# Two edits to a graph-plus-LSTM kernel: the short item chunk as one stacked pass, and a fourth input pass between the two groups' state matmuls

## The reference

```
x = x + relu(adj @ (item_feat @ W_item.T + b_item) + layernorm(x) @ W_user.T + b_user)
h = lstm(layernorm(x))                      # 10000 steps in the reference, 128 wide, 4 gates
g = argmax(h @ W_lin.T + b_lin)             # 0 or 1 for each row
w = g * h;  inc = cumsum(w)
x = x + 2*h + (inc - w) * fw_att + (inc[-1] - inc) * bw_att
```

## Time and profile before

| | |
|---|---|
| median of 3 runs | 1486.9 us (1485.9 to 1490.18) |
| the profiled execution, its own time | 1486.99 us |
| its span, first to last instruction | 1485.2 us |
| granted TensorE clock over the span | 0.990 |
| PE busy | 1449.2 us (98%) |
| DVE busy | 1218.3 us (82%) |
| ACT busy | 1088.3 us (73%) |
| DMA moved | 426.67 MB, mean 287 GB/s |
| stage 1 (PE's last `psG` pass starts) | to 1169.8 us |
| stage 2 and the closing sums | the rest |

### The profile page before, as it was taken

One profiled execution on the slowest core, in us unless ns is written; L12 is line 12 of the kernel. 1 busy time (PEld: TensorE's weight loads), 2 busy tenths in 40 slices (PEclk: granted clock), 3 DMA queues, 4 the chain that ended last, 5 costly groups with the idle time before them and its releaser, 6 DMA issues.

```text
span 1485.2 us, 25012 instructions
## 1 busy us (share of the span) xinstructions
PE 1449.2 (98%) x7584; PEld 1227.4 (83%) x7584; DVE 1218.3 (82%) x2027; ACT 1088.3 (73%) x1601; POOL 212.8 (14%) x189
## 2 busy tenths in 40 slices
PE   8999999999999999999999999999999799999994
PEld 7878888788778888888888888877888699999994
DVE  7998888888888888888888888888888566677677
ACT  5778777778777778777777787777778476556662
POOL 0000010000001001001001000000100032017775
PEclk9999999999999999999999999999999899999997
DMA  9889999999999999999999999999999203000003
GB/s 382 309 325 359 376 345 360 367 350 365 358 352 361 370 351 363 371 356 358 367 352 371 352 359 376 340 369 355 350 363 380 97 1 123 15 2 0 0 0 139
DMA packets 70515, 426.67 MB, mean 287 GB/s; under 512 B 8723, under 2 KB 17620, under 8 KB 70358
## 3 DMA queue, kind: packets, MB, share of 16 engines
q1 hardware_dynamic: 68896, 425.12, 76.6%
q10 hardware_dynamic: 1590, 1.18, 0.2%
HBM read 416.02 MB, written 10.24 MB: 287 GB/s over the span
## 4 chain that ended last, share of the span: by engine, by line
issue 79%; PE 19%; DVE 1%; POOL 0%; ACT 0%; POOLq 0%; DVEq 0%
PE psZ L848 10%; PE psZ L836 3%; PE psZ L837 2%; PE psZ L838 2%; PE psZ L854 1%; DVE u L1241 1%; PE psZ L824 0%; PE psZ L914 0%; POOL rstd L419 0%; POOLq L422 0%; ACT normed L557 0%; PE psZ L918 0%; DVE dif L1256 0%; PE psV L734 0%; DVE dif L1254 0%
## 5 line engine op out<-in xcount | busy, mean ns | idle before, releaser
L998 DVE TENSOR_TENSOR a_lo<-raw,a_hi 128x1000 fp32r<-128x1000 f32 (+1 forms) x800 | 917.3, 1182 | 108.4 <-ACT a_hi L586 101.9
L586 ACT ACTIVATE a_hi<-raw 128x1000 fp32r<-128x1000 f32 (+1 forms) x800 | 806.2, 1030 | 253.7 <-PE psG L759 170.6
L757 PE MATMUL psG<-a_hi,item_hi 128*128 128x500 f32 (+1 forms) x1580 | 635.5, 402 | 2.5 <-DVE a_lo L998 1.6
L759 PE MATMUL psG<-a_hi,item_lo 128*128 128x500 f32 (+1 forms) x1580 | 615.6, 390 | 0.0
L758 PE MATMUL psG<-a_lo,item_hi 128*128 128x500 f32 (+1 forms) x1580 | 612.2, 387 | 0.0
L757 PEld LDWEIGHTS psG<-a_hi,item_hi 128*128 128x128 f32 (+1 forms) x1580 | 296.4, 188 | 81.1 <-DVE a_lo L998 16.7
L759 PEld LDWEIGHTS psG<-a_hi,item_lo 128*128 128x128 f32 (+1 forms) x1580 | 297.7, 188 | 61.1
L758 PEld LDWEIGHTS psG<-a_lo,item_hi 128*128 128x128 f32 (+1 forms) x1580 | 297.3, 188 | 60.7 <-issue 4.4
L419 POOL TENSOR_TENSOR rstd<-var,minus_half 125x4 f32<-125x4 f32 x40 | 76.2, 1905 | 1096.8 <-DVE var L982 1096.8
L848 PE MATMUL psZ<-hist,wh 128*128 (+1 forms) x1264 | 169.8, 277 | 0.1
L848 PEld LDWEIGHTS psZ<-hist,wh 128*128 128x128 f32 x1264 | 154.0, 191 | 2.1 <-issue 0.6
(11 more groups left out here) (143 smaller groups left out, 809.4 us busy)
## 6 DMA issues: line engine op xcount, KB each, us to landing
raw<-in_adj_main SPq DMA_DIRECT2D x360, 1000.0 KB, 6.9
raw<-in_adj_main SPq DMA_DIRECT2D x40, 750.0 KB, 4.2
x_copy<-xb SPq DMA_DIRECT2D x20, 250.0 KB, 5.5
u<-x_copy SPq DMA_DIRECT2D x1, 5000.0 KB, 14.8
out<-u SPq DMA_DIRECT2D x25, 200.0 KB, 2.4
xb<-in_xT SPq DMA_DIRECT2D x18, 250.0 KB, 5.3
u<-in_itemT SPq DMA_DIRECT2D x8, 512.0 KB, 11.7
u<-in_itemT SPq DMA_DIRECT2D x1, 648.0 KB, 12.5
```

What stands on the lines that cost most here:

```text
L586: nc.scalar.activation(a_hi[:, s % CUT, 0:n], raw[:, r % RAW, at:at + n], ACT.Copy)\
L757: pe.matmul(bank, w_hi, hi, start=(c == 0), stop=False)
L759: last = pe.matmul(bank, w_lo, hi, start=False, stop=(c == CH))
L998: dve.tensor_tensor(a_lo[:, s % CUT, 0:n], raw[:, r % RAW, at:at + n], a_hi[:, s % CUT, 0:n].bitcast(f32), ALU.subtract).then_inc(lo_ready, 1)
```

## The change

Part one, the short chunk. The DMA of its 16 rows is issued three times, to partitions 0, 32 and 64 (`STACK`). ACT rounds all of them as before. DVE splits only the full chunk into `a_lo`, and then, on partitions 32 to 47, overwrites the rounded values by the rests. The item weights of the chunk are laid out the same way once, in block 0: high part on partitions 0 and 32, low part on 64, zeros between. PE then does one pass over 80 partitions, in which the three products add up by themselves, in place of three passes over 16.

Part two, the LSTM. The twelve input passes become a list; four of them, instead of three, stand between the state matmuls of group 0 and group 1, and eight instead of nine after those of group 1.

More of the change, by code:

```diff
@@ L134, in program @@
         bi_row = sb("bi_row", [1, HID], f32, first)
+        item_tail = sb("item_tail", [P, STACKED], f32, first)
         item_lo = sb("item_lo", [P, (CH + 1) * HID], f32r, first)
@@ L200, in program @@
         wi_in = sem("wi_in")
+        item_tail_ready = sem("item_tail_ready")
         bi_in = sem("bi_in")
@@ L420, in inv_std @@
                                    ALU.pow).then_inc(ln_rstd, 1)
-            with nc.gpsimd.Fori(0, 2 * NB) as m:
+            inv_std(0)
[5 more added lines that the diff above has]
+            with nc.gpsimd.Fori(1, 2 * NB) as m:
                 inv_std(m)
@@ L797, in item_quad @@
                     pe.wait_ge(item_sum, q - 1)
+                if q == QUADS - 1:
+                    pe.wait_ge(item_tail_ready, 1 + len(STACK))
                 for c in range(4 * q, min(4 * q + 4, CH + 1)):
-                    rows = P if c < CH else TAIL
-                    last = pe.matmul(psI[0:rows, q % 2, (c % 4) * HID:(c % 4 + 1) * HID],
-                                     u[:, L + c * P:L + c * P + rows], wi[:, :], start=True, stop=True)
+                    rows = P if c < CH else STACKED
+                    columns = u[:, L + c * P:L + (c + 1) * P] if c < CH else item_tail[:, :]
+                    last = pe.matmul(psI[0:rows, q % 2, (c % 4) * HID:(c % 4 + 1) * HID], columns, wi[:, :],
+                                     start=True, stop=True)
                 last.then_inc(item_psum, 1)
@@ L835, in from_input @@
                     z = psZ[:, 2 * par + q // 2, (q % 2) * XC:(q % 2 + 1) * XC]
-                    pe.matmul(z, w_hi, hi, start=(q % 2 == 0), stop=False, skip_group_check=True)
-                    pe.matmul(z, w_hi, lo, start=False, stop=False, skip_group_check=True)
-                    pe.matmul(z, w_lo, hi, start=False, stop=False, skip_group_check=True)
+                    if part == 0:
+                        pe.matmul(z, w_hi, hi, start=(q % 2 == 0), stop=False, skip_group_check=True)
+                    if part == 1:
+                        pe.matmul(z, w_hi, lo, start=False, stop=False, skip_group_check=True)
+                    if part == 2:
+                        pe.matmul(z, w_lo, hi, start=False, stop=False, skip_group_check=True)
             def from_state(n, g, row, par):
@@ L878, in lstm_pair @@
                          logit=lambda: logits(2 * i + half, par, half))
-            pe.wait_ge(prep, 14)
+            pe.wait_ge(prep, 17)
             pe.wait_ge(u_ready, NB)
@@ L1014, in item_sum_part @@
                 dve.wait_ge(prep, 1)
-                for c0, c1, rows in ((0, n - 1, P), (n - 1, n, TAIL)):
-                    dve.tensor_tensor(sq[0:rows, c0 * HID:c1 * HID].rearrange("p (c h) -> p c h", h=HID),
-                                      psI[0:rows, q % 2, c0 * HID:c1 * HID].rearrange("p (c h) -> p c h", h=HID),
-                                      bi[0:rows, :].unsqueeze(1).to_broadcast([rows, c1 - c0, HID]), ALU.add)\
-                        .then_inc(item_sum if rows == TAIL else prep, 1)
-                dve.wait_ge(prep, 2)
+                for c0, c1, a, b in ((0, n - 1, 0, P), *((n - 1, n, a, a + TAIL) for a in STACK)):
+                    dve.tensor_tensor(sq[a:b, c0 * HID:c1 * HID].rearrange("p (c h) -> p c h", h=HID),
+                                      psI[a:b, q % 2, c0 * HID:c1 * HID].rearrange("p (c h) -> p c h", h=HID),
+                                      bi[a:b, :].unsqueeze(1).to_broadcast([b - a, c1 - c0, HID]), ALU.add)\
+                        .then_inc(item_sum if a == STACK[-1] else prep, 1)
+                dve.wait_ge(prep, 4)
             def item_lo_part(q):
```

27 lines of the change are left out of this document (14 added, 13 removed).

## The result

The changed kernel takes 1474.64 us in the median of four runs (1470.58 to 1476.14), the kernel before 1488.02 (1485.9 to 1490.18): ratio 0.9906, 95% interval 0.988 to 0.9931. Forecast were 1470.6, range 1464 to 1480. The profiled execution took 1475.1 us with a span of 1473.2, against 1486.99 and 1485.2 before: 11.9 us less, 16.4 were forecast. The main mechanism came as forecast, but the sum holds one gain that wasn't foreseen and four losses that were missed or put too small.

What follows compares the result with a forecast made beforehand. PE's own passes were taken to set the pace. Stage 1 (16.0 saved, 0.8 and 1.0 lost: -14.2) and the LSTM (-2.2) took 1486.99 us to 1470.6, range 1464 to 1480.

Steps and rivals of the forecast that it cites:

- The block end, 0.84 us: End of each block: one 80-row pass replaces three 16-row ones, saving PE 0.84 us a block, 16.0 over 19.
- rival (a): Block end: 80 rows still cost the change of rows, 8.6 us saved instead of 16.0, total 1478.0; chance 0.15.
- I price it at nothing: Two added short-chunk DMAs a block: landing at most 0.55 us later, covered by a 0.83 us margin, no cost.
- rival (d): Block end: the two added small DMAs lag 1.05 us each, 0.43 lost a block, total 1493.8; chance 0.05.
- I take 1.0 us over all blocks as loss (bounds 0 and 5): Stage 1, nearly full DMA engines: PE's waits for DVE splits grow, costing 1.0 us over all blocks.
- 0.5 later. Enough.: Next block's first DVE split ends at 714.10, PE would arrive at 714.62, 0.5 us later; no new wait.
- Rival (c): Stage 1: the DMA queue is the real bound, blocks keep 56.70 us plus 0.18, total 1489.0; chance 0.07, part included.
- 0.8 us, bounds 0.4 and 1.2: Block 0: added DVE work (two adds, the operation on own_hi, the split in two) costs 0.8 us.
- block 0's 0.84 is lost: Join to block 1: PE already waits 1.42 us for DVE's first split, so block 0's 0.84 us saves nothing.
- The fourth input pass: LSTM loop: fills a 0.10 us stall in group 1's state matmuls (S1); step 3.33 to 3.23, 2.2 us gained.
- From the first logits on nothing moves: LSTM second half: state is ready over 0.7 us before group 0's state matmuls (S0), so steps gain nothing.
- Rival (b): LSTM loop: no slack behind group 0's state matmuls (S0); 1.6 us slower instead of 2.2 faster, total 1474.4; chance 0.09.

Runs made afterwards that it cites:

- The run with the weight operations moved: Changed kernel with VectorE's twelve operations on the weights moved from block 0's end to pieces 12 to 17 of the last block: 1470.8 us, ratio 0.9886.

## Why the prediction was right, and which terms were off

**The block end, 0.84 us: right.** 80 rows run like 128, and rival (a) falls. The 0.84 is 2 x 0.225 for two passes and 0.39 for the change of rows; taken apart, two passes are 0.48 a block (56.07 with three stacked passes, 55.59 with one) and the change of rows 0.33 to 0.39 (the old passes over 80 rows, the stacked one over 48 and 64).

**Not foreseen: 0.27 us a block inside the blocks,** 19 x 0.27 = 5.1 us. All four kernels with PE's old passes at the block end (before, the loads alone, the four passes alone, the old passes over 80 rows) have 0.2267 to 0.2269 between passes; all nine with the stacked pass have 0.2256 or 0.2257, with one pass or three, 48 rows or 80. Not the number of passes, not the rows, not the added loads. What is left is all that the nine share: where instructions stand in a program, VectorE's last split, which is cut in two, GpSimd's added work, and the place of the tiles in SBUF, for the change allocates a new tile `item_tail`, 320 bytes a partition, ahead of `item_lo`, `raw`, `a_hi` and `a_lo`. That the pattern of distances comes back with each turn of the rings `a_hi` and `a_lo` would fit the last; no run tests it. The cause stays open.

**"I price it at nothing" (the two added DMAs): right.** Alone they change nothing measurable, and rival (d) falls. ACT's wait for the short chunk grew by 0.6 us, a little over the 0.55 allowed. The trace counts 64 more packets a block, not 32, half of them under 512 bytes. The 2.0 us that the prediction takes from the Trainium skill, "DMA: Bandwidth & Descriptors", Anatomy of one DMA, stand there for DMAs that GpSimd issues. These are SyncE's, and whatever fixed time they have, two more of them a block cost the run nothing: it isn't serial in the queue.

**"I take 1.0 us over all blocks as loss (bounds 0 and 5)": this is the step that failed most.** It measured 7.5 us (4 to 11 by the other profiles of this stage). The prediction worked out that 1.7 us of each block were free in the queue and that 0.84 + 0.18 would fit. It was 1.11 + 0.18, and above all a free mean is not a free queue: with less time per block, the loads are late more often, mostly at the same places of the block. ACT's waits for loads went from 67 to 123 us while its waits for PE fell from 158 to 97; with 5% fewer bytes the two turned back. "0.5 later. Enough." for the first split of the next block left 0.17 us over the 0.35 that was known to be enough, and in 5 of 18 block ends that split came late, by 0.1 to 0.2 us. Rival (c), that the queue keeps blocks at 56.70, is wrong as it stood, for many blocks take 55.59; but its mechanism holds for part of the gain.

**"0.8 us, bounds 0.4 and 1.2" (block 0): mis-sized.** It measured 1.5. Of this 1.3 us are shown in the rows: the two added sums cost 0.6 and not 0.4, the operation on `own_hi` 0.4 and not 0.3, the split in two 0.2 and not 0.1. And "block 0's 0.84 is lost" left out what a longer wait does to PE: the clock fell, 1.5 us more in block 1. The run with the weight operations moved takes away both the wait and the fall.

**The fourth input pass: right.** Forecast were S1 with 1.05, S0 to S1 1.37, S1 to S0 1.86, the step 3.23 and 2.2 us in all; measured were 1.05, 1.38, 1.86, 3.24 and 2.5 in the steps that it was to shorten. "24 of 32 steps" was too careful: the mean over the loop fell from 3.32 to 3.24, and only one step of the 32 kept the old period. (3.33 - 3.23 is 0.10; the prediction went on with 0.09.) "From the first logits on nothing moves" was wrong by 0.7 us, in all kernels with the stacked pass, and that makes the 1.9 of the whole stretch. Rival (b) had 0.35 as the least that S0 needs behind its state; with four passes it is 0.21 to 0.24 in the 32 steps.

Sum of the stage, forecast and measured: block ends -16.0 and -15.6 (19 x 0.82), inside the blocks 0 and -5.1, block 0 +0.8 and +1.5, and its own block end saved nothing in both; clock 0 and +1.5, loads +1.0 and +7.5: -14.2 and -10.2 (10.1 by the rows). LSTM: -2.2 and -2.5, and +0.7 unforeseen. The mechanism of both edits was right. That the time came so close is in part luck: an unforeseen gain of 5 met unforeseen losses of 9.4, and without that gain the sum would have come to 1480, the upper edge of the range.

## What to carry to other kernels

A short last chunk can cost more than its passes: with 16, 48 or 64 rows it took 0.33 to 0.39 us for going there and back. Running it over 80 rows with zeros in the weights took that away without any stacking. Here PE was the bound and the DMA engines were at 0.97, and a gain in PE was paid out only in part: ask which waits for loads there are already, and count on more of these (here nearly twice as many), not on the mean that is free. Weigh a wait of PE not by its length alone: those of 2.2 to 2.7 us here took the clock with them, those of 1.4 to 1.6 did not. And when a pace changes where nothing was edited, compare all kernels that you have, stretch by stretch: that showed here that the LSTM's 1.9 us were 2.5 gained and 0.7 lost.

## What was unexpected in the hardware

- In eight profiles PE stood still for 2.2 to 2.7 us at the end of block 0, and the granted clock fell to 0.50 for 3.4 us, 0.0 to 1.1 us after PE was back; in six it stood for 1.6 us or less, and the clock stayed at 1.00.
- The same full passes of 128 x 500 follow each other at a mean of 0.2268 us in one program and 0.2256 in another, in a pattern with a period of 24 passes that is one in the nine kernels with the stacked pass and another in the four without. In the LSTM 38 unchanged steps took 138.8 us in the kernels with the old short passes and 139.5 in those with the stacked one. Both causes are open.
- A pass over 48 or 64 rows costs the same change of rows as one over 16, to within some 0.05 us.
